# One core, a four-layer model: all of x3 loaded in the last expert turn, scatter-adds of a group with one wait, first expert weights loaded in the layer before, last additions shared by VectorE and GpSimd

## What is computed

```python
probs = softmax(xf @ Wg);  topv, topi = top_k(probs, 2);  gates = topv / sum(topv)
pos   = rank of the token within its expert;  keep = pos < cap        # cap = 2151 rows per expert
h     = gelu(expert_in @ W1 + b1);  y = h @ W2 + b2                   # 8 experts, 256 -> 1024 -> 256
out   = sum over the token's two experts of gate * y
x     = x3 + layernorm(out)
```

## Time and profile before

| | |
|---|---|
| median of 3 timed runs | 4602.2 us (4597.26 to 4608.24) |
| the profiled execution | 4610.1 us, span 4608.3 us |
| busy over the span | PE 89%, PEld 68%, DVE 61%, ACT 41%, POOL 26% |
| mean granted TensorE clock | 0.942 |
| HBM read, written | 85.92 MB, 86.65 MB |

### The profile page before, as it was taken

One profiled execution on the slowest core, in us unless ns is written; L12 is line 12 of the kernel. 1 busy time (PEld: TensorE's weight loads), 2 busy tenths in 40 slices (PEclk: granted clock), 3 DMA queues, 4 the chain that ended last, 5 costly groups with the idle time before them and its releaser, 6 DMA issues. The chain is left out here.

```text
span 4608.3 us, 78285 instructions
## 1 busy us (share of the span) xinstructions
PE 4088.1 (89%) x26868; PEld 3115.5 (68%) x26868; DVE 2812.6 (61%) x8170; ACT 1910.7 (41%) x3047; POOL 1191.9 (26%) x1096
## 2 busy tenths in 40 slices
PE   4999999999993899999999999999999599989990
PEld 2344444444442788888888888888888498989890
DVE  4787777887862665555565655555655455556554
ACT  1565666666662333343243333332332233333322
POOL 3243333433422211111111111111111133333334
PEclk8899989999985999999999999999999699999995
DMA  3442443353322000000000000000000133333335
GB/s 71 84 88 54 76 100 55 73 112 76 54 51 90 4 17 14 19 19 15 14 15 16 15 13 13 15 13 4 13 13 9 62 60 63 64 61 67 61 65 200
DMA packets 168272, 222.45 MB, mean 48 GB/s; under 512 B 26732, under 2 KB 143435, under 8 KB 167872
## 3 DMA queue, kind: packets, MB, share of 16 engines
q1 hardware_dynamic: 139840, 180.74, 17.0%
q0 software_dynamic: 25728, 28.03, 4.0%
q10 hardware_dynamic: 2304, 8.39, 0.4%
HBM read 85.92 MB, written 86.65 MB: 37 GB/s over the span
## 5 line engine op out<-in xcount | busy, mean ns | idle before, releaser
L787 ACT ACTIVATE probs<-a_scores 128x1024 f32<-128x1024 f32 (+3 forms) x768 | 615.3, 811 | 376.9 <-PE a_scores L691 370.2
L948 DVE CUSTOM_DVE_ANT_0 a_scores<-a_scores,mask 128x384 f32<-128x384 f32 (+3 forms) x1024 | 482.1, 515 | 121.4 <-PE a_scores L677 115.4
L691 PEld LDWEIGHTS a_scores<-q_st,k_st 50*128 50x128 f32 x1536 | 151.4, 194 | 411.6 <-issue 282.0
L252 POOL TENSOR_TENSOR l_ln_rstd<-l_ln_ve,minus_half 128x4 f32<-128x4 f32 x80 | 84.0, 1050 | 1230.9 <-DVE l_ln_ve L225 1230.7
L691 PE MATMUL a_scores<-q_st,k_st 50*128 50x512 f32 (+3 forms) x1536 | 354.8, 460 | 33.5 <-issue 24.7
L951 DVE TENSOR_REDUCE mx<-a_scores 128x2 f32<-128x1024 f32 x256 | 311.0, 1224 | 118.0 <-PE a_scores L677 116.9
L711 PE MATMUL a_out<-probs,v_aug 128*32 128x512 f32 (+3 forms) x3072 | 352.1, 533 | 1.9 <-POOL probs L880 1.8
L677 PE MATMUL a_scores<-k_st,q_st 48*128 48x512 f32 (+3 forms) x1536 | 309.5, 401 | 45.8 <-ACT probs L787 28.1
L2377 POOL DMA_INDIRECT expert_sums_scratch<-e_y,e_number x136 | 224.0, 1647 | 376.2 <-DMA expert_sums_scratch<-e_y,e_number 325.9
L880 POOL TENSOR_SCALAR_AFFINE_SELECT probs<-probs 128x512 f32<-128x512 f32 x256 | 162.6, 636 | 567.1 <-ACT probs L787 563.6
L2308 PE MATMUL e_out<-e_weights_lo,e_hT_hi 128*128 128x256 f32 x1088 | 308.4, 283 | 0.0
(11 more groups left out here) (259 smaller groups left out, 10228.6 us busy)
## 6 DMA issues: line engine op xcount, KB each, us to landing
q_st<-parts SPq DMA_DIRECT2D x192, 128.0 KB, 4.5
k_st<-parts SPq DMA_DIRECT2D x192, 128.0 KB, 6.2
expert_rows_scratch<-empty_row SPq DMA_DIRECT2D x8, 2210.0 KB, 14.3
e_weights<-in_L_ffn_W_dram SPq DMA_DIRECT2D x16, 1024.0 KB, 7.7
e_rows<-expert_rows_scratch SPq DMA_DIRECT2D x24, 390.0 KB
e_rows<-expert_rows_scratch SPq DMA_DIRECT2D x16, 520.0 KB
x_in<-in_L_attn_x_dram SPq DMA_DIRECT2D x8, 1024.0 KB, 6.9
expert_sums_scratch<-empty_row SPq DMA_DIRECT2D x8, 1024.0 KB, 15.9
```

Of the source, the lines that this page charges most:

```text
L691: last = nc.tensor.matmul(psum_r[:, R.slot(u), h2, 0:w], k_st[rows, 2 * hg + pair, i * P:(i + 1) * P], q_st[rows, 2 * hg + pair, q0:q0 + w ...
L787: nc.scalar.activation(probs[:, k % 3, 2 * pair:2 * pair + 2, 0:w], psum_r[:, R.slot(u), :, 0:w], ACT.Exp).then_inc(R.evacuated[R.slot(u)], 1)
L948: last = nc.vector.tensor_tensor_reduce(s, s, mask[:, HALF - w:HALF], 1.0, LEAST, ALU.add, ALU.max, out[:, h2, :])
```

## The change

1. *Weights early.* The places of `held`, the raw weights and the split weights are laid out below the linear layer's tiles. In the linear layer's last group SyncE, once that group's query and key products are made, loads expert 0's weights into the raw place. In the experts, a group's rows are loaded ahead of the biases.
2. *x3 whole.* All 16 groups of x3 are loaded in the last expert turn, four behind each of the last four rows loads: 6 into `held`, 4 into the raw weights' place, 6 into places of the seventh expert's split weights. The combine loads no x3.
3. *Scatters.* GpSimd waits once per group, not after each scatter. So that the free slots of one group do not add into the same spare rows, `sums_dram` has 512 spare rows and `empty` four rows; clear_rows issues four DMAs of four tiles and one for the sums, two more and the spare rows' own come after the first turn, and none at the end.
4. *Additions.* In the combine VectorE adds the even groups and GpSimd the odd ones. VectorE's order is statistics(2k), statistics(2k + 1), addition(2k); GpSimd's is power(2k), addition(2k - 1), power(2k + 1).

```diff
@@ softmax layer
 def clear_rows(b):
-    sp.dma_start(zv[bass.ds(b, 1), ...], empty[:, :]... .broadcast_to([P, SLOTS // P // B, RW]))
+    for f in range(PER):
+        sp.dma_start(zv[bass.ds(b * PER + f, 1), :, :, :]..., fours).then_inc(zeroed, 16)
...
 turn(0, GU_FIRST, True, False, True)
+for f in range(B * PER, FOURS):
+    sp.dma_start(zv[f], fours).then_inc(zeroed, 16)
+sp.dma_start(sums_dram[N:N + SPARE * P, :]..., empty[:, :, 0:D]).then_inc(zeroed, 16)
...
 sp.wait_ge(x2_stored, B * 16)
-sp.dma_start(sums_dram[N:N + P, :], empty[:, 0:D]).then_inc(zeroed, 16)
@@ linear layer, SyncE's group
 store(g - 1, 1 - s)
+if last:
+    G.wait_full(sp, g, U["QK"] + NQK - 1)
+    load_weights(sp, W1, W2, 0, raw_e, e_loaded)
@@ experts, SyncE
+def hold(i, seq, q):
+    first = (q - (NQ - 4)) * 4
+    if first == 4:
+        sp.wait_ge(lo_ready, count(i, seq, ("W", 1, NW - 1)))
+    elif first == 8:
+        YU.wait_full(sp, i, 2 * NGR - 1)
+    for g in range(first, first + 4):
+        sp.dma_start(held_group(g)..., xv[g]).then_inc(x3_held, 16)
...
 sp.dma_start(rows[:, 0:n, :], ...).then_inc(rows_loaded, 16)
+if q % NGR == 0:
+    biases()
...
+if not more and q >= NQ - 4:
+    hold(i, seq, q)
@@ experts, GpSimd
-    pool.wait_ge(added, i * (2 * CT * 16) + (e2 * CT + t0 + j + 1) * 16)
-    pool.sem_inc(begun, 1)
+pool.wait_ge(added, i * (2 * CT * 16) + (e2 * CT + t0 + n) * 16)
@@ combine
+def finish(g):                       # GpSimd
+    pool.wait_ge(normed, g + 1)
+    nc.gpsimd.tensor_tensor(y[:, g, :, :], y[:, g, :, :], held_group(g), ALU.add
+                            ).then_inc(out_ready[1], 1)
 for g in range(NG):
     lns[g % LNS].power(pool, 0, g // LNS)
+    if g % 2 == 0 and g > 0:
+        finish(g - 1)
+finish(NG - 1)
...
 for g in range(NG):                  # VectorE
     dve.wait_ge(y_loaded[g % LOADS], 16 * (g // LOADS + 1))
+    if g >= LNS:
+        dve.wait_ge(normed, g - LNS + 1)
     lns[g % LNS].variance(...)
-    if g >= LAG:
-        finish(g - LAG)
+    if g % 2 == 1:
+        finish(g - 1)
```

More of the change, by code:

```diff
@@ L142, in build, with held_group, load_weights @@
                           weight, disha, x2_dram, rows_dram, sums_dram)
-        linear_layer(nc, ident, minus_half, spot, x2_dram, g1, be1, Wq, Wk, Wv, Wo, g2, be2, Wf1, Wf2, Wg,
[L144 to L148, removed]
+        with ExitStack() as ctx:
+            held = ctx.enter_context(nc.sbuf_tensor("x3_held", [P, HELD, G4, D], F32))
+            with nc.sbuf_tensor("x3_in_weights", [P, IN_RAW, G4, D], F32) as in_raw:
+                pass
+            raw = ctx.enter_context(nc.sbuf_tensor("e_weights", [P, NW, HALF], F32))
+            with nc.sbuf_tensor("x3_in_high", [P, IN_HI, G4, D], F32) as in_hi:
+                pass
+            parts = {"hi": ctx.enter_context(nc.sbuf_tensor("e_weights_hi", [P, 2, NW, HALF], F32R))}
+            with nc.sbuf_tensor("x3_in_low", [P, IN_HI, G4, D], F32) as in_lo:
+                pass
+            parts["lo"] = ctx.enter_context(nc.sbuf_tensor("e_weights_lo", [P, 2, NW, HALF], F32R))
+        def held_group(g):
+            for tile, n in ((held, HELD), (in_raw, IN_RAW), (in_hi, IN_HI)):
+                if g < n:
+                    return tile[:, g, :, :]
+                g -= n
+            return in_lo[:, g, :, :]
+        raw_loaded = [whole.enter_context(nc.semaphore(name)) for name in ("e_w1_loaded", "e_w2_loaded")]
+        linear_layer(nc, ident, minus_half, spot, x2_dram, g1, be1, Wq, Wk, Wv, Wo, g2, be2, Wf1, Wf2, Wg,
+                     x3_dram, rows_dram, W1, W2, raw, raw_loaded)
+        sb("x3_held_place", [P, HELD, G4, D])
+        sb("e_weights_place", [P, NW, HALF])
+        sb("e_weights_parts_place", [P, 2, 2, NW, HALF])
+        experts(nc, ident, rows_dram, raw, parts, raw_loaded, W1, b1, W2, b2, sums_dram, x3_dram,
+                held_group)
+        combine(nc, minus_half, sums_dram, held_group, out_rows)
+def load_weights(sp, W1, W2, e, raw, raw_loaded):
+    for n, w in enumerate((W1, W2)):
+        sp.dma_start(raw[:, n * (NW // 2):(n + 1) * (NW // 2), :].rearrange("p k n -> p (k n)"),
+                     w[bass.ds(e, 1), :, :].rearrange("a (c p) n -> p (a c) n", p=P)
+                     ).then_inc(raw_loaded[n], 16)
 def token_rows(dram):
@@ L2092, in _, with experts @@
                     locate(NGR - 1, step)
-def experts(nc, ident, rows_dram, W1, b1, W2, b2, sums_dram, x3_dram, held):
+def experts(nc, ident, rows_dram, raw, w, raw_loaded, W1, b1, W2, b2, sums_dram, x3_dram, held_group):
     MH = HE // P
@@ L2140, in experts @@
         psum_y = ctx.enter_context(nc.psum_tensor("e_out", [P, 2, HALF], F32))
-        raw = sb("e_weights", [P, NW, HALF])
-        w = {part: sb(f"e_weights_{part}", [P, 2, NW, HALF], F32R) for part in ("hi", "lo")}
         b1_sb = sb("e_b1", [P, 2, MH])
```

84 lines of the change are left out of this document (33 added, 51 removed).

## The result

Measured beside each other, the kernel before took 4605.22 us (median, 4597.26 to 4611.91) and the changed one 4578.09 us (4570.3 to 4583.71): a ratio of 0.9938, 95% interval 0.992 to 0.9956. A second measurement with more executions gave 4602.96 (4593.01 to 4616.31) and 4572.18 us (4557.61 to 4582.23), ratio 0.9932 [0.9913, 0.9951]. That is 27 to 31 us less; the forecast was 30.8 less.

The account below looks back on a forecast made before the run. TensorE works almost without a break from 3664 to 4502 us, so gains lie in idle seams: -2.1 - 6.6 - 19.9 - 3.7 + 1.5 = -30.8 from 4602.2 gives 4571.4 us, range 4561 to 4589.

Parts of the forecast that it names:

- End of the softmax layer: Seam before the linear layer: without the last clearing DMA behind the last x2 store, the barrier opens 2.1 us sooner.
- Cost of the clearing in the turns: Softmax layer turns: each batch's clearing becomes four DMAs instead of one, but SyncE has room; value 0.
- Start of the experts: Start of the expert block: first expert's weights loaded early let casts start with the block; 6.6 us less (5 to 7).
- Scatters: Experts' end: with one wait per group, scatters follow 1.86 us apart, so the last stage's first load comes 19.9 us sooner.
- Turn boundaries: Between expert turns: VectorE's last evacuations wait less for GpSimd's backlog; 3.7 us less, from 0 to 5.
- x3 held whole: Last expert turn: sixteen x3 loads instead of six may delay scatters, but GpSimd has room; value 0, at most +5.
- Last stage: Combine: removing x3 loads gains 0; sharing additions gives circles of 8.0 us instead of 7.93; 1.5 us more in all.
- served one at a time: Rival at the experts' scatters: landing time grows by what the waits took, leaving only -7.2, 4595.0 us; chance 8%.
- SyncE held by clearing: Rival in the softmax layer: four clearing DMAs fill the queue, minus_max comes late, every turn pays; over 4611.4 us; chance 3%.
- not early: Rival on the first expert's weights: SyncE's wait in the linear layer's last group comes late; then -24.2, 4578; no chance given.
- a circle of 9 or more: Rival in the last stage: VectorE and GpSimd exclude each other, taking back 8.5 us more, giving 4580; no chance given.
- The lock: Last stage: a two-SBUF-input VectorE instruction and a GpSimd one reading SBUF exclude each other; by this the stage gains nothing.

Follow-up runs that it names:

- clear_last: Changed kernel with the clearing of the spare rows' sums moved back behind the softmax layer's last store; 4574.14 us, ratio 0.9938 to the kernel before.
- waits_back: Changed kernel with a wait after every accumulating scatter again; 4599.42 us, ratio 0.9989 to the kernel before.
- shared_lag2: Changed kernel with additions still shared between VectorE and GpSimd, but two groups behind their statistics; 4569.57 us, ratio 0.9921 to the kernel before.
- rows_first: Against the kernel with all additions on VectorE two groups behind, four statistics sets: second rows load issued before the next weights; 4561.63 us, ratio 0.9908.
- lag2_x3_loaded: Against the kernel with all additions on VectorE two groups behind, four statistics sets: ten x3 groups loaded in the last stage; 4562.79 us, ratio 0.9908.

## Why the prediction was right

It was right in the total and in the order of the terms. Each term against its stretch in the table:

- *End of the softmax layer*, -2.1: measured -1.75 (9.57 to 7.82), and clear_last shows the cause. Cost of the clearing in the turns, put at 0: none was found. Its issue takes 5.64 us of SyncE's time against 6.00, and the layer's end moved only within the variation.
- *Start of the experts*, -6.6: measured -6.8 and, by undoing it alone, -6.5. Below it lay what I had listed as a fact and not priced: weights ahead of the second rows (3.2 us).
- *Scatters*, -19.9: measured -20.4. Spacing 1.87 us (forecast 1.86), last scatter's start to first load 5.78 (5.79). The rule "the landing time does not grow with three in flight" was the risk, and it held.
- *Turn boundaries*, -3.7 (0 to 5): this is the term that was too small. TensorE's waits at the three boundaries were 31.6 and 29.8 us together in the two profiles of before, and 25.9 in the mean of the nine without the waits: -4.8. Its whole expert work went from 839.5 to 833.9: -5.6. At the first two boundaries, where I had 1.7, undoing the waits gives back 2.5 (21.4 us together in waits_back, 18.8 in the mean of the nine). At the last one, where I had 2.0, it is 9.5 and 9.2 us before and 7.1 in the nine: the size was right. But it is 6.7 in waits_back, so the waits alone don't bring it back, and I had put it on them. GpSimd let VectorE go 1.1 and 0.7 us behind TensorE's last matmul of the turn in the two profiles of before, and 1.6 us ahead of it in waits_back: some other edit left GpSimd less far behind there. Which one wasn't tried.
- *x3 held whole*, 0 and at most +5: 0. One of four bursts held up a scatter, in both profiles (7.30 us in the second), and GpSimd had made it up before the end. In the first:

```profile
4429.03 1.56 POOL L2427 DMA_INDIRECT expert_sums_scratch<-e_y,e_number  x1 [6.96 <-issue]
```

- *Last stage*, +1.5: measured +1.1 and +0.7. In the second pair of profiles the last addition starts 68.1 us after the first load (68.6 before), and from its start to the end it is 5.5 instead of 4.3, GpSimd's addition being longer. In the circle the sum held by GpSimd's addition ended at 7.12, where I had 7.2, since that addition began a little sooner; the small sums behind it took 0.62 us, not 0.8, so the circle is 7.74 and not 8.0. In the kernel before I named the addition at 4588.16 as the one that closes the circle; it waited for nothing. The one that waited is at 4584.73, behind the power at 4580.32 that VectorE's addition had stretched to 1.99 us. Both run at the same 7.93 us, so the forecast did not suffer.

The rule of the Trainium skill ("SBUF — State Buffer", section "Who interferes with whom") that of a VectorE instruction with two SBUF inputs and a GpSimd one that reads SBUF the later is fully blocked agrees with the trace: 0.17 us became 1.10 in the changed kernel and 2.33 in shared_lag2, each time ending with GpSimd's addition. It holds for four elements a partition too.

Of the rivals, "served one at a time" was refuted by the 1.87 us spacing and by waits_back; "SyncE held by clearing" by the turns; "not early" by 17.7 us; a circle of 9 or more by 7.74. The lock is on the path all the same: 1.10 us for a sum of 0.17 in the changed kernel, and in shared_lag2 two groups take 1.03 us more than with all additions on VectorE.

By these stretches (means over the profiles) the change is worth 1.75 + 6.7 + 5.6 + 20.3 - 0.9 = 33.5 us less, of which the medians show 27 to 31. The rest is within the variation of the first two layers. That the second measurement gave the 30.8 of the forecast to the tenth is luck.

Where there was time left: the last stage's ten loads and its shared additions, two of the named parts: taking the loads away gained nothing, and sharing cost 0.9 us. What paid there, 10.0 us, was the distance between an addition and its statistics, together with the four sets of tiles. With the circle open the kernel takes 0.9899 of the time before; no kernel that was run is faster, and rows_first and lag2_x3_loaded (both 0.9908) are on par.

## What to carry to other kernels

Cost a seam by the chain that crosses it and check it by that stretch of the profile; a total that differs by 16 us between two executions of one kernel can't confirm a step of 2. Where no engine of a stage is busy throughout, look for a circle of latencies before moving work or bytes: one group more of distance, with tiles enough for it, took 10 us off a stage that neither fewer loads nor a second engine had shortened. Read from the idle time in front of each instruction which wait closes the circle: here it moved from the additions to the statistics with the change. Split elementwise work onto GpSimd only if VectorE has none of its own in the same moments, however small: beside an addition of 2.35 us there a sum of 0.17 took 2.33, and the 2.2 us lost were more than the 1.14 that the addition saved.

## What the runs showed of the hardware that I had not expected

- Accumulating indirect DMAs of one group, 1.87 us apart, with the next waiting for none before it: GpSimd's next gate waited 2.51 us for the last of them, and 2.59 where each had had a wait of its own.
- A full DMA (share 1.02, 411 GB/s for 20 us) of loads and stores together held up no engine (VectorE was busy for 19.38 of each 20 us); each load was issued groups ahead of its use, the last one of x3 17.8 us ahead.
- A rows load that took 3.8 us from issue to use with no weights in front of it took 7.0 behind a load of weights issued 3.3 us earlier.
- The same kernel had a granted clock of 0.90 in one execution and 0.96 in another over the same 342 us of the softmax layer, and that layer ended 20 us apart.
